# An attention and top-2 expert kernel on one core: 24 expert blocks moved under the gating of the last token groups, with a table of their own, and a smaller mask

## The chip, the cores and the metric

The kernel runs on one core of a Trainium2 chip. The core has a matrix engine (TensorE, PE in the views), VectorE (DVE), ScalarE (ACT), GpSimd (POOL) and SyncE (SP, which here only issues transfers). They run unsynchronised and meet through semaphores. Matmuls write to PSUM, everything else lives in SBUF or in device memory. The metric is the device time of the whole program in microseconds, lower is better; the number compared is the median of several runs.

## The reference

Only what matters here is left in. 128 sequences of 64 tokens, width 128, so 8192 tokens.

```python
def attention(q, k, v, mask, ...):            # q = layernorm(x), k = v = ctx
    qp = (q + pe) @ Wq.T + bq; kp = (k + pe) @ Wk.T + bk; vp = v @ Wv.T + bv    # 16 heads of 8
    scores = jnp.einsum('bhqd,bhkd->bhqk', qh, kh) * d_head ** (-0.5)
    m = mask[:, None, None, :] | causal[None, None, :, :]
    scores = scores - m.astype(scores.dtype) * 10000000.0
    out = softmax(scores) @ vh
    return out @ Wo.T + bo

def ffn(x, ...):                              # x = layernorm(x1)
    probs = softmax(gelu(x @ wg1 + bg1) @ wg2)          # 8 experts
    top_vals, top_idx = jax.lax.top_k(probs, 2)
    h = gelu(einsum('nd,edh->enh', x, w_in))            # 128 -> 256
    o = einsum('enh,ehd->end', h, w_out)                # 256 -> 128
    return einsum('ne,end->nd', gates, o)

x = x + attention(...)
x = x + ffn(layernorm(x))
```

## The kernel before

It has two phases. The **attention phase** walks over 64 tiles of 128 tokens (`NT`), in 16 stages (`NS`) of four tiles. For a tile, PE makes the scores of all 16 heads in two PSUM banks and adds the mask (`scores`, L377 and L383), DVE takes the row maxima (L776) and subtracts them (L780), ACT exponentiates (L620), PE transposes the probabilities (L393), ACT copies them out (L678), PE multiplies by the values (L406, L411), DVE divides (`normalise`, L788, L790), PE applies Wo (`project_o`, L420) and DVE adds the residual (L798). Each engine has one hand-written order: for every stage a `body` with steps u = 0 to 3, in which the work of other stages is slotted. Two to three stages later the same bodies do the **gating** of a group (the four tiles of a stage r): layer norm, transposes (`transpose_rows`, L444), hidden layer (`gate_hidden`, L450), Gelu (L668), logits (L456), softmax (L672, L830 to L832), the two largest experts (`find_two_largest`, `select`), the rank of each token among those of its pair of experts (`rank_tokens`, L463 to L470), the running counts (`count_tokens`, L865, L869) and the row number of each token (`positions`). POOL then scatters the group's rows (`scatter_rows`, L1136, four DMAs) into `routed_rows` in device memory. That buffer has one region for each of the 28 pairs of experts.

When the last two groups (14 and 15) are through, the final counts are copied (`tails`, L1026). From them SP and ACT each write 14 paddings of 128 rows behind the ends of the regions (`pad_regions`, L231 loads the addresses into registers, L238 issues), and `make_tables` on DVE works out for each block of 128 rows where it begins and which two experts it needs.

The **expert phase** runs over 91 blocks (`NB`, a static bound). SP loads each block of rows (`load_group`, L330, up to `RX` = 8 blocks ahead), PE transposes it (L553), PE does the up projection (L562) from the weights that ACT has copied to a fixed place (L732), ACT applies Gelu (L717), PE does the down projection (L573), DVE combines with gates and residual (L1055, L1059), POOL scatters the result to the output (L1174). PE's order in the loop is up(b+1), transposes(b+2), down(b). The mask of a stage is loaded to 128 partitions with all eight sequences of the stage for each of them (L260) and made into `negmask` by one DVE instruction over 128x512 elements (L770), although each partition belongs to one sequence of each tile only. It is added with four matmuls of 64x64, one for each quarter of the array.

```python
for half in range(2):
    r = slice(half * 64, half * 64 + 64)
    for b in range(2):
        last = nc.tensor.matmul(S_bank[half][b * L:(b + 1) * L, :]..., spread_s[r, r],
                                negmask[r, par, 2 * u + b, :]..., start=False, stop=True)
```

## Time and profile before

| | us |
|---|---|
| median of 3 runs | 621.63 (619.68 to 622.26) |
| the profiled execution | 623.75 |
| its span, first to last instruction | 622.0 |
| attention phase and last gating, to the final counts | 0 to 411.3 |
| paddings, tables, first block on its way | 411.3 to 432.4 |
| expert phase | 432.4 to 622 |

The profiled execution lies 2.1 us above the median, and 1.75 us of it are outside the span. The page gives PE 81% busy over the span, DVE 77%, ACT 63%, POOL 40%, but these are averages over phases with different limits: in the page's slices DVE shows nines through the attention phase, PE shows nines through the expert phase, and between them both fall to zero while the DMA engines are at their busiest. The granted TensorE clock is 9 in nearly all slices and 5 in the three slices of the transition.

### The profile page before, as it was taken

Reading aid. Unit: us, or ns where it says so; the run is one execution under the profiler, and the core shown is the slowest. Engines: PE = TensorE matmul, PEld = TensorE weight load, DVE = VectorE, ACT = ScalarE, POOL = GpSimd, SP = SyncE. Lnnn points to the kernel's source line nnn. Section 1 sums busy time; section 2 is a strip of 40 time slices with the busy share of each in tenths; the row PEclk is TensorE's granted clock in tenths of the full one; section 3 lists DMA queues with packets and bytes.
Section 4 is the critical chain, followed back from the end, with each engine's and each line's share of the span. In section 5 each row is a group of like instructions: output and inputs, shape, how many; then the busy total and the mean of one; then the engine's idle time right before and its main releaser. Section 6 shows DMA issues by size and latency. Waiting matters only on the chain.

```text
span 622.0 us, 18994 instructions
## 1 busy us (share of the span) xinstructions
PE 501.8 (81%) x6640; PEld 377.4 (61%) x6640; DVE 481.1 (77%) x1629; ACT 393.0 (63%) x723; POOL 248.8 (40%) x323
## 2 busy tenths in 40 slices
PE   2579898888888888888888887411999999999992
PEld 0146555555554554554555554301999999999992
DVE  3588999999999999999999997660566666566662
ACT  2156687777777777777777676511666666566660
POOL 4131233353353354254254233340355555455552
PEclk9999999999999999999999999555999999999997
DMA  3137212212212212212110101047233334333310
GB/s 110 18 81 220 62 48 69 78 42 66 81 40 65 83 39 65 83 40 62 46 41 26 52 20 38 35 137 241 76 107 103 109 105 110 98 110 86 80 42 1
DMA packets 41805, 46.87 MB, mean 75 GB/s; under 512 B 9738, under 2 KB 33555, under 8 KB 41248
## 3 DMA queue, kind: packets, MB, share of 16 engines
q1 hardware_dynamic: 33696, 30.39, 18.7%
q0 software_dynamic: 5984, 12.90, 6.1%
q10 hardware_dynamic: 2032, 2.36, 1.3%
q8 instruction: 55, 0.90, 0.6%
q14 instruction: 38, 0.31, 0.2%
HBM read 28.54 MB, written 18.58 MB: 76 GB/s over the span
## 4 chain that ended last, share of the span: by engine, by line
DVE 35%; PE 34%; issue 13%; SPq 9%; DMA 2%; ACT 2%; POOL 1%; ACTq 0%; another core or an unknown queue 0%; POOLq 0%; DVEq 0%
PE probs_t L562 14%; PE bank L573 13%; DVE smax L776 9%; DVE rden L788 7%; SPq L266 5%; DVE rows L798 2%; PE scores L553 2%; DVE left L843 2%; DVE sm L780 1%; SPq L238 1%; DVE stat L753 1%; DVE stat L804 1%; DVE xT L763 1%; PE scores L377 1%; PE probs_t L393 1%
## 5 line engine op out<-in xcount | busy, mean ns | idle before, releaser
L1174 POOL DMA_INDIRECT out<-yb,token_row x91 | 89.3, 982 | 106.2 <-DVE yb L1059 65.9
L1136 POOL DMA_INDIRECT routed_rows<-rows,pos x64 | 64.3, 1004 | 122.5 <-DVE pos L879 100.9
L678 ACT ACTIVATE pt<-probs_t 128x1024 f32<-128x1024 f32 x64 | 65.5, 1023 | 60.0 <-PE probs_t L393 59.7
L717 ACT ACTIVATE hb<-probs_t 128x512 f32<-128x512 f32 x91 | 54.3, 597 | 73.2 <-PE probs_t L562 54.9
L562 PE MATMUL probs_t<-xbT,wi 128*128 128x128 f32 x728 | 98.1, 278 | 2.3 <-ACT wi L732 1.2
L377 PE MATMUL scores<-kx,qT 64*64 64x512 f32 x512 | 70.6, 621 | 36.2 <-DVE sm L780 23.9
L573 PE MATMUL bank<-wo,hb 128*128 x728 | 96.1, 275 | 0.0
L562 PEld LDWEIGHTS probs_t<-xbT,wi 128*128 128x128 f32 x728 | 90.1, 195 | 3.1 <-issue 1.7
L573 PEld LDWEIGHTS bank<-wo,hb 128*128 128x128 f32 x728 | 88.5, 192 | 0.1
L776 DVE TENSOR_REDUCE smax<-scores 128x16 f32<-128x1024 f32 x64 | 77.8, 1216 | 12.2 <-PE scores L383 10.9
L780 DVE TENSOR_TENSOR sm<-scores,smax 128x1024 f32<-128x1024 f32 x64 | 78.4, 1224 | 2.2
L1055 DVE SCALAR_TENSOR_TENSOR part<-bank,gate,xb 128x128 f32<-128x128 f32 x91 | 31.8, 350 | 59.4 <-issue 32.1
L732 ACT COPY wi<-wi_all 128x256 f32 x182 | 63.8, 401 | 18.6 <-issue 18.6
L393 PE MATMUL probs_t<-ident_s,sm 128*128 128x128 f32 x512 | 67.3, 274 | 1.3 <-ACT sm L620 1.3
L620 ACT ACTIVATE sm<-sm 128x1024 f32<-128x1024 f32 x64 | 67.3, 1051 | 0.2
L788 DVE RECIPROCAL rden<-bank 128x128 f32<-128x128 f32 x64 | 60.1, 940 | 2.3 <-remote 2.0
L393 PEld LDWEIGHTS probs_t<-ident_s,sm 128*128 128x128 f32 x512 | 57.2, 141 | 5.6 <-issue 4.9
L406 PEld LDWEIGHTS bank<-pt,vx 128*32 128x32 f32 x2048 | 32.0, 109 | 45.6 <-DVE onT L790 29.2
L406 PE MATMUL bank<-pt,vx 128*32 128x64 f32 x2048 | 41.9, 222 | 18.1 <-DVE onT L790 7.8
L377 PEld LDWEIGHTS scores<-kx,qT 64*64 64x64 f32 x512 | 13.8, 132 | 69.0 <-DVE sm L780 41.3
L411 PE MATMUL bank<-pt,ones_s 128*32 128x128 f32 x1024 | 43.2, 275 | 0.6 <-issue 0.5
L1035 DVE COPY xbT<-scores 128x128 f32<-128x128 f32 x91 | 26.0, 286 | 20.2 <-PE scores L553 18.5
(117 smaller groups left out, 838.3 us busy)
## 6 DMA issues: line engine op xcount, KB each, us to landing
xb<-routed_rows SPq DMA_DIRECT2D x91, 132.5 KB
ctx_in<-ctx_t SPq DMA_DIRECT2D x16, 256.0 KB, 3.0
x_all<-x SPq DMA_DIRECT2D x16, 256.0 KB, 3.3
kx<-kT SPq DMA_DIRECT2D x256, 16.0 KB
routed_rows<-padding_rows SPq DMA_DIRECT2D x15, 132.5 KB
routed_rows<-padding_rows ACTq DMA_DIRECT2D x14, 132.5 KB
out<-yb,token_row POOLq DMA_INDIRECT x91
mask_in<-mask SPq DMA_DIRECT2D x16, 64.0 KB, 3.8
```

What stands on the lines that cost most here:

```text
L377: nc.tensor.matmul(S_bank[half][b * L:(b + 1) * L, :].rearrange("p (h k) -> p h k", k=L), qT[r, par, o:o + L], kx[r, par, :, o:o + L], sta ...
L393: last = nc.tensor.transpose(PT_bank[j // 4][:, (j % 4) * P:(j % 4 + 1) * P], pr[:, j * P:(j + 1) * P], ident[:, :])
L406: nc.tensor.matmul(XB[g * VB:(g + 1) * VB, b * L:(b + 1) * L], v[:, c:c + VB], pt[:, 2 * g + j, b * L:(b + 1) * L], start=(j == 0 and b == ...
L562: last = nc.tensor.matmul(UBK[b % 2][:, (2 * j + c) * BLK:(2 * j + c + 1) * BLK], wi[:, b % RH, j, c * P:(c + 1) * P], xbT[:, b % RH, :], ...
L573: last = nc.tensor.matmul(DBK[b % 2][:, j * D:(j + 1) * D], hb[:, b % RH, 2 * j + c, :], wo[:, bass.ds(experts[j], 1), c, :].rearrange("p ...
L620: nc.scalar.activation(sm[:, u % 2, :, :], sm[:, u % 2, :, :], ACT.Exp).then_inc(s_exp, 1)
L678: nc.scalar.activation(pt[:, :, :].rearrange("p j q -> p (j q)"), PT2[:, :], ACT.Copy).then_inc(s_ptev, 1)
L776: nc.vector.reduce_max(smax[:, :], S2[:, :].rearrange("p (h k) -> p h k", k=L), AX).then_inc(s_max, 1)
L780: nc.vector.tensor_tensor(sm[:, u % 2, :, :], S2[:, :].rearrange("p (h k) -> p h k", k=L), smax[:, :].unsqueeze(2).broadcast_to([P, H, L]) ...
L788: nc.vector.reciprocal(rden[:, :], XB[:, P:2 * P]).then_inc(s_rden, 1)
L1136: nc.gpsimd.indirect_dma_start(out=rows_d, out_offset=bass.IndirectOffsetOnAxis(ap=pos[:, r % RR, u:u + 1], axis=0), in_=rows[:, r % RR, u ...
L1174: nc.gpsimd.indirect_dma_start(out=out, out_offset=bass.IndirectOffsetOnAxis(ap=token_row[:, b % RY:b % RY + 1], axis=0), in_=yb[:, b % RY ...
```

## The change

**The first 24 blocks come early.** After group 12 is counted there are enough rows in `routed_rows` for at least 24 full blocks, whatever the input. In stage 15 DVE makes a first table from the counts so far, rounded down to full blocks (`blocks_of_bins(0)`, `ends_of_bins(0)`, `bins_of_blocks(0)`, `write_tables(0)`, `start_second_part`); PE turns it (`turn_table(0)`). The expert loop then starts after the hidden layer of group 14, and the rest of the gating of groups 14 and 15 is written into the loop by block number (`last_gates(b)` on PE, ACT and DVE; `SCATTER_AT` on POOL). The second table, of 67 blocks, follows at blocks 11 to 14. The number of blocks stays 91.

**The paddings** are all issued by SP, 14 before the loads of blocks 16 to 19 and 14 before those of blocks 20 to 23 (`PADS_BEFORE`), after `tails`, which DVE copies at block 10.

**The mask** is loaded with two DMAs a stage, each to 64 partitions, and kept once: `negmask` is 128x256, and two full matmuls of 128x128 by 512 columns add it.

**Around it**: x is kept in a ring of six stages instead of whole, `RX` goes from 8 to 10, `RY` from 6 to 10, at the end of the attention `normalise(63)` on DVE and `project_o(63)` on PE go ahead of other work.

```diff
+EARLY = 13
+NA = 24
+PART_OF = (0, NA)
+NBS = (NA, NB - NA)
+PADS_BEFORE = (4, 5)
-RX = 8
+RX = 10
-RY = 6
+RY = 10
+SCATTER_AT = (4, 12)
...
-                    sp.dma_start(mask_in[:, s % RING, :, :], mask[s * 2 * U:(s + 1) * 2 * U, :].partition_broadcast(P)
-                                 ).then_inc(s_m[s % RING], 16)
+                    for b in range(2):
+                        src = mask[s * 2 * U:(s + 1) * 2 * U, :].rearrange("(u b) k -> b u k", b=2)[b]
+                        sp.dma_start(mask_in[b * L:(b + 1) * L, s % RING, :, :], src.partition_broadcast(L)
+                                     ).then_inc(s_m[s % RING], 16)
...
-                sp.wait_ge(s_tails, 1)
-                pad_regions(mybir.EngineType.SP, sp, PAD_SP)
-                sp.wait_ge(s_tabd, 1)
                 for g in range(len(GROUPS)):
+                    if g in PADS_BEFORE:
+                        if g == PADS_BEFORE[0]:
+                            sp.wait_ge(s_tails, 1)
+                        half = PADS_BEFORE.index(g)
+                        pad_regions(range(half * NP // 2, (half + 1) * NP // 2))
                     load_group(g)
...
                     for half in range(2):
-                        r = slice(half * 64, half * 64 + 64)
-                        for b in range(2):
-                            last = nc.tensor.matmul(S_bank[half][b * L:(b + 1) * L, :].rearrange("p (h k) -> p h k", k=L),
-                                                    spread_s[r, r], negmask[r, par, 2 * u + b, :].unsqueeze(1).broadcast_to([L, HH, L]),
-                                                    start=False, stop=True)
+                        last = nc.tensor.matmul(S_bank[half][:, :].rearrange("p (h k) -> p h k", k=L), spread_s[:, :],
+                                         negmask[:, par, u, :].unsqueeze(1).broadcast_to([P, HH, L]),
+                                         start=False, stop=True)
...
+                def last_gates(b):
+                    if b == 0:
+                        pe.wait_ge(s_res, NT)
+                        gate_logits(NS - 2)
+                    if b == 3:
+                        pe.wait_ge(s_rge, NS - 1)
+                        transpose_rows(NS - 1)
+                        pe.wait_ge(s_lsh, NS - 1)
+                        rank_tokens(NS - 2)
+                    if b == 5:
+                        gate_hidden(NS - 1)
+                    if b == 7:
+                        pe.wait_ge(s_pch, CNT * (NS - 2) + 2)
+                        gate_logits(NS - 1)
+                    if b == 10:
+                        pe.wait_ge(s_lsh, NS)
+                        rank_tokens(NS - 1)
+                    if b == 13:
+                        turn_table(1)
...
+                def last_gates(b):
+                    if b == 0:
+                        gate_exp(NS - 2)
+                        ln2_norm(NS - 1)
+                    if b == 3:
+                        xt2_evac(NS - 1)
+                    if b == 5:
+                        gate_gelu(NS - 1)
+                    if b == 7:
+                        gate_exp(NS - 1)
...
-                act.wait_ge(s_tails, 1)
-                pad_regions(mybir.EngineType.Activation, act, PAD_ACT)
...
+                def last_gates(b):
+                    if b == 0:
+                        choose(NS - 2)
+                    if b == 3:
+                        count_tokens(NS - 2)
+                        positions(NS - 2)
+                    if b == 7:
+                        choose(NS - 1)
+                    if b == 10:
+                        count_tokens(NS - 1)
+                        dve.wait_ge(s_pch, CNT * (NS - 1) + 2)
                         nc.vector.tensor_copy(tails[:, :], run_s[:, :]).then_inc(s_tails, 1)
+                        positions(NS - 1)
+                    if b == 11:
+                        blocks_of_bins(1)
+                        ends_of_bins(1)
+                    if b == 12:
+                        bins_of_blocks(1)
+                    if b == 14:
+                        write_tables(1)
```

Where instructions stand, at the places that matter. On **SP**, before the change, the last paddings are followed by the register load of the first four blocks' addresses and the loads of blocks 0 to 3 (`ISA` rows move an address from a register; `xb<-routed_rows` is the load of a block):

```order
L238 DMA routed_rows<-padding_rows 16x2120
L318 TENSOR_LOAD row_table
L330 ISA
L330 DMA xb<-routed_rows 128x265
```

In the changed kernel, blocks 0 to 15 are loaded first. These are the rows from the end of the first 14 paddings over block 16 to 19 to the second register load of counts:

```order
L326 DMA routed_rows<-padding_rows 16x2120
L333 TENSOR_LOAD row_table
L346 ISA
L346 DMA xb<-routed_rows 128x265
L346 ISA
L346 DMA xb<-routed_rows 128x265
L346 ISA
L346 DMA xb<-routed_rows 128x265
L346 ISA
L346 DMA xb<-routed_rows 128x265
L319 TENSOR_LOAD tails
```

What moved: the paddings stood ahead of every block load, and stand now ahead of block 16 and, after these four loads, once more ahead of block 20. The shape of a padding transfer is the same on both sides.

On **ACT**, before the change, the gating of group 15 ends, the paddings follow (L238), and then the loop begins; these are the rows up to the first padding (`ex` is the exponential of the logits, `rows` the normed rows of a group, `hid_s` the hidden layer's Gelu):

```order
L672 ACT_TABLE_LOAD
L672 ACTIVATE ex<-lg 128x32
L641 ACTIVATE rows<-rows,shift,rstd 128x128 x4
L643 ACTIVATE rows<-routing_s 128x4
L662 ACTIVATE xt<-bank 128x512
L668 ACT_TABLE_LOAD
L668 ACTIVATE hid_s<-bank,bg_s 128x128
L672 ACT_TABLE_LOAD
L672 ACTIVATE ex<-lg 128x32
L231 TENSOR_LOAD tails
```

In the changed kernel the same place reads as follows, from the Gelu of block 0 to that of block 1 (`hb<-probs_t` is a block's Gelu, `wi<-wi_all` a copy of expert weights):

```order
L753 ACTIVATE hb<-probs_t 128x512
L704 ACT_TABLE_LOAD
L704 ACTIVATE ex<-lg 128x32
L673 ACTIVATE rows<-rows,shift,rstd 128x128 x4
L675 ACTIVATE rows<-routing_s 128x4
L770 ISA
L770 COPY wi<-wi_all 128x256
L770 ISA
L770 COPY wi<-wi_all 128x256
L753 ACT_TABLE_LOAD
L753 ACTIVATE hb<-probs_t 128x512
```

What moved: the exponential of group 14 and the layer norm of group 15 stand between the Gelu of block 0 and the weight copies of block 2.

## Rows read from the trace of the kernel before

**Rows 1.** Busy time by stretch: start:end, length, engines, PEclk, DMA share, GB/s.

```profile
84.00:384.00 300.00, 255.84 (x4136) 160.62 (x4133) 288.41 (x848) 226.76 (x360) 118.83 (x172) 1.00 0.19 53
440.00:611.00 171.00, 169.05 (x1512) 168.63 (x1510) 106.75 (x538) 105.07 (x263) 87.39 (x90) 1.00 0.34 93
```

**Rows 2.** Chain that ended last, in the transition: start us, us, what.

```profile
411.46 1.15 SPq L231
...
421.43 0.50 SPq L238
...
422.11 0.50 SPq L238
...
425.50 4.61 DMA routed_rows<-padding_rows
430.27 2.15 DMA xb<-routed_rows
```

**Rows 3.** The same chain in the attention phase: mask on SP, PE and DVE.

```profile
33.13 0.50 SPq L260
...
71.62 0.22 PE scores L383 x4
...
99.54 0.60 DVE negmask L770
```

**Rows 4.** Timeline, end of the attention: start, us, engine line op out<-in [idle before <-releaser].

```profile
388.12 0.96 DVE L788 RECIPROCAL rden<-bank 128x128 f32<-128x128 f32 x1 [1.95 <-remote]
...
395.94 0.77 PE L420 MATMUL bank<-wo_s,onT 128*128 128x128 f32 x2 [0.75 <-DVE onT L790]
...
413.17 1.08 DVE L905 TENSOR_TENSOR cum<-cum 128x28 f32<-128x28 f32 x5
```

**Rows 5.** Timeline of the gating of group 15, and ACT's way into the loop.

```profile
400.22 1.65 ACT L641 ACTIVATE rows<-rows,shift,rstd 128x128 f32<-128x128 f32 x4 [1.30 <-POOL shift L1126]
...
402.11 1.09 PE L444 MATMUL bank<-ident_s,rows 128*128 128x128 f32 x4 [4.38 <-ACT rows L643]
...
403.23 0.60 ACT L662 ACTIVATE xt<-bank 128x512 f32<-128x512 f32 x1 [1.27 <-PE bank L444]
...
403.84 1.28 ACT L668 ACT_TABLE_LOAD   x1
...
405.14 0.37 ACT L668 ACTIVATE hid_s<-bank,bg_s 128x128 f32<-128x128 f32 x1
...
406.82 0.23 ACT L672 ACTIVATE ex<-lg 128x32 f32<-128x32 f32 x1
...
409.69 0.27 DVE L856 TENSOR_TENSOR sel<-code,routing_s 128x112 f16<-128x112 f32 x1
...
425.67 1.42 ACT L732 COPY wi<-wi_all 128x256 f32 x4 [18.62 <-issue]
```

**Rows 6.** Timeline of PE in the expert phase: blocks 0, 1 and 20.

```profile
433.48 2.04 PE L562 MATMUL probs_t<-xbT,wi 128*128 128x128 f32 x8 [0.54 <-DVE xbT L1035]
...
438.02 1.06 PE L573 MATMUL bank<-wo,hb 128*128 x8
...
441.70 0.27 PE L553 MATMUL scores<-ident_s,xb 128*128 128x128 f32 x1
...
472.04 0.27 PE L553 MATMUL scores<-ident_s,xb 128*128 128x128 f32 x1
```

**Rows 7.** Busy time of PE alone by stretch: length, PE (count), PEclk, DMA share, GB/s.

```profile
388.00:390.00 2.00, 0.54 (x36) 0.99 0.19 68
390.00:392.00 2.00, 1.09 (x27) 0.50 0.00 0
...
436.00:438.00 2.00, 1.78 (x9) 0.56 0.02 7
```

**Rows 8.** Instructions by line: duration ns min/median/max, first and last start us.

```profile
L231 SPq TENSOR_LOAD <-tails x2: 1152/1314/1477, 411.5 to 419.8; - x2
...
L318 SPq TENSOR_LOAD <-row_table x23: 295/302/675, 426.1 to 591.8; - x23
...
L722 ACTq TENSOR_LOAD <-expert_table x23: 547/637/787, 425.0 to 599.1; - x23
```

More of the change, by code:

```diff
@@ L44 @@
 RW = 2 * D + E + 1
[L45 removed]
+ROUND = float(3 << 22)
 CH = 9
@@ L226, in build @@
         s_tok, s_part = (sem(n) for n in ("token_rows_ready", "first_expert_added"))
-        PAD_SP, PAD_ACT = range(0, NP // 2), range(NP // 2, NP)
-        def pad_regions(engine, queue, bins):
-            for first in range(bins.start, bins.stop, NP // 4):
-                _, values = nc.values_load_multi_w_load_instructions(
-                    tails[0:1, first:first + NP // 4], engines=[engine], min_val=0, max_val=ROWS - BLK,
-                    skip_runtime_bounds_check_because="made on the chip by counting into existing regions")
-                for k in range(NP // 4):
-                    start = (first + k) * REG
-                    at = nc.s_assert_within(values[k], start, start + N,
-                                            skip_runtime_bounds_check_because="a region holds all tokens")
-                    queue.dma_start(rows_d[bass.ds(at, BLK), :], pad_c.ap()).then_inc(s_pad, 16)
         (s_bt, s_bte, s_up, s_gl, s_dn, s_gm, s_gt, s_yb) = (sem(n) for n in (
@@ L313, in _, with pad_regions @@
                     body(s, s // 2, s % 2)
+                def pad_regions(bins):
+                    for first in range(bins.start, bins.stop, NP // 4):
+                        _, values = nc.values_load_multi_w_load_instructions(
+                            tails[0:1, first:first + NP // 4], engines=[mybir.EngineType.SP], min_val=0, max_val=ROWS - BLK,
+                            skip_runtime_bounds_check_because="made on the chip by counting into existing regions")
+                        for k in range(NP // 4):
+                            start = (first + k) * REG
+                            at = nc.s_assert_within(values[k], start, start + N,
+                                                    skip_runtime_bounds_check_because="a region holds all tokens")
+                            sp.dma_start(rows_d[bass.ds(at, BLK), :].rearrange("(a r) w -> a (r w)", a=16),
+                                         pad_c.ap().rearrange("(a r) w -> a (r w)", a=16)).then_inc(s_pad, 16)
                 def load_group(g):
-                    first, n = GROUPS[g]
+                    p, first, n = GROUPS[g]
+                    if first == PART_OF[p]:
+                        sp.wait_ge(s_tabd, 3 * p + 1)
                     _, values = nc.values_load_multi_w_load_instructions(
@@ L472, in rank_tokens, with turn_table @@
                     last.then_inc(s_rank, 1)
+                def turn_table(p):
+                    pe.wait_ge(s_spread, p + 1)
+                    for k in range(3):
+                        last = nc.tensor.transpose(TABLE[p][:, k * P:(k + 1) * P], spread_out[:, k, :], ident[:, :])
+                    last.then_inc(s_tabp, 1)
                 def body(s, i, par):
@@ L499, in body @@
                             project_v(s + 1)
+                        if u == 2 and s == NS - 1:
+                            turn_table(0)
                         if u == 0:
@@ L736, in _ @@
                 act.wait_ge(s_wo, 32)
-                act.wait_ge(s_tabd, 2)
-                for g, (first, n) in enumerate(GROUPS):
+                for g, (p, first, n) in enumerate(GROUPS):
                     experts = experts_of(g)
@@ L1007, in _ @@
                     body(s, s // 2, s % 2)
+                normalise(NT - 1)
                 residual(NT - 2)
@@ L1164, in body @@
                             add_positions(s + 3)
-                        if u == 3 and runs(s, 3):
+                        if u == 3 and runs(s, 3, NS - 2):
                             scatter_rows(s - 3, (3,))
```

198 lines of the change are left out of this document (104 added, 94 removed).

## The prediction

> **What bounds the kernel now.** I read the busy time by stretch first [rows 1]. From 84 to 384 us DVE is busy 288.4 of 300: the attention phase is DVE-bound once it is under way. From 440 to 611 PE is busy 169.1 of 171: the expert phase is PE-bound, at 1.896 us a block (sixteen blocks lie between the transposes of block 4 at 441.70 and of block 20 at 472.04, which is 30.34 us [rows 6]). Between them the chain of waits [rows 2] runs through SP: the counts are there at 411.46, paddings are issued until 425.99, the last one lands at 430.11, the first block lands at 432.42. PE has nothing to do for these 21 us, and it is thinly busy through the gating before. That hole, 37.5 us from the last `project_o` at 395.94 [rows 4] to the first up projection at 433.48 [rows 6], is the time in which nothing of the expert phase runs. The question is how much of it comes back as waits inside the expert loop.
>
> I sum against the profiled execution: span 622.0, time 623.75, which is 2.1 above the median of 621.63. I carry differences in the span over to the median.
>
> **Attention phase, the mask.** DVE's mask instruction costs 0.60 us of its chain [rows 3]. Half the elements saves 0.26 of it (the full one is 679 ns for 512 columns, a 128-column one on these engines some 0.29, so 256 columns are about 0.42). It is on the DVE-bound path in about 12 stages: -3.1 us. Against it stand two things. SP, which is the chain in the first 64 us, issues one more mask load of about 0.54 (0.50 and the gap [rows 3]) for each of stages 2 to 4: +1.6, up to +3 because the pieces are now 64 bytes. And the four mask matmuls take 0.22 beyond the scores [rows 3], because four 64x64 quarters stream side by side; two full ones stream one after the other, about 0.43. DVE reaches the maxima 1 to 3 us after the scores are done in a steady stage, so this +0.21 a tile is hidden by DVE's other work, except in the four tiles around 70 to 85 us where the chain runs through PE: +0.8. If DVE's cover were gone it would cost 64 x 0.21 = 13 us. Sum: **-0.5**, bounds -3 and +3.
>
> The Trainium skill, page "TensorEngine Tiling (Array Packing)", says that 64x64 mode gives four independent tiles. By that rule this edit gives speed away on PE. The 0.22 in the row agrees; it changes the sum only by the tiles on the PE path.
>
> **Stage 15, the early table.** DVE gets 6 + 5 + 4 small operations at about 0.22 (five took 1.08 [rows 4]) before the last subtraction, with the spread of 384 elements 3.7 us in all, then 1.7 us for writing the tables and starting the second part. The 3.7 lie on DVE's bound path. The 1.7 and part of the rest fall where DVE waits anyway: it stood 1.95 for an unseen cause before the reciprocal at 388.12 [rows 4]. `normalise(63)` now goes ahead of the count, which saves 1.5. Following the order through, the last `project_o` ends at 397.3 instead of 396.7 (395.94 + 0.77), bounds 395 and 399.
>
> **Into the loop.** From there: transposes of group 14 1.09, copy 0.60, table load 1.28, Gelu 0.37 [rows 5], load of eight registers 0.64 [rows 8], two weight copies 0.71 (half of 1.42 for four [rows 5]), and 0.2 of hops: the up projection of block 0 starts at T = **402.2**, not 433.48. That is 31.3 us won so far. The first blocks' rows are ready: POOL's last scatter of group 12 is shifted by the same 3.7 us, to about 390, which is ten ahead of need.
>
> **The loop under the gating.** Without gating, the down projection of block 0 ends 5.6 us after T (439.08 - 433.48 [rows 6], at half clock for the most part) and that of block 10 ends 19.0 later. Now follow ACT, since PE's up(b+2) waits for ACT's weight copies and its down(b+1) for ACT's Gelu.
> - Block 0: ACT waits for down(0), the logits (0.4) and DVE (0.8), then exponential 0.23, layer norm 1.65 + 0.2, copies 0.71, table load 1.28, Gelu 0.60. down(1) starts 6.2 us after down(0) ends instead of 0.95: +5.2. 3.8 us of it leave PE with nothing.
> - Block 3: transposes 1.09, copy 0.60, copies 0.71, Gelu 0.60 and hops: +2.5. Block 5: hidden layer 0.43, Gelu 0.37: +1.4. Block 7: logits, DVE, exponential, copies, table load, Gelu: +3.3, and DVE's choice of experts (2.9 us, from the exponential's end at 407.05 to 409.96 [rows 5]) another 0.2.
> - Clock. The granted clock fell to 0.50 (1.2 GHz) at 390 after PE was busy 0.54 of 2 us, and came back just before 438 (0.56 over 436 to 438) [rows 7], some 4 us after the first up projection. I expect it to fall in block 0's gap: +1.7.
>
> down(10) ends at T + 5.6 + 19.0 + 12.6 + 1.7 = T + 38.9, and rank, count and copy put `tails` at T + 40.4 = 442.6. In the kernel before it was 411.4.
>
> About table loads the Trainium skill ("ScalarE: Activation LUTs", on what ACT_TABLE_LOAD costs) gives 1283 ns and a drain of 1380 ns more for each switch. The rows show 1.28 us between a copy that ended at 403.83 and a Gelu at 405.14, with no drain. By the page the two exposed switches would add 2.8 us.
>
> **The paddings, now in the loop.** This decides it. SP waits for `tails` before it loads block 16. Then 14 paddings: two register loads (1.15 and 1.48 [rows 8]) and 14 issues. With ACT's queue silent, an issue comes every 0.68 us (421.43 to 422.11 [rows 2]), which makes 12.1 us; the row of before, both queues and pauses included, is 14.5 for 14 (411.46 to 425.99). I take 12.9, near the lower end, as the rival queue is gone but not every pause of the first seven need be its doing. Register load and gap 0.4, block 16 is issued at 13.3 and lands 2.15 later [rows 2], at T + 56. PE needs it in iteration 14, about T + 48 after the second table's work on DVE (4 to 5 us over blocks 11 to 14): PE stands some 7 us. After the four loads (1.9) come 14 more paddings, 12.9, and 0.4: block 20 is issued at T + 40.4 + 13.3 + 1.9 + 13.3 = T + 68.9 and lands at T + **71.1** = 473.3. PE has had work for only four blocks in between (8 to 10 us) and stands again for about 5. DVE's table work and one wait are covered by the other; this chain alone sets the time.
>
> Before, PE transposed block 20 at 472.04 [rows 6]. So the chain is **1.3 us behind** the old kernel here, and all 31.3 us are spent. I expect the clock to fall in both waits. The first recovery hides in the second wait, the second one does not: about 5 us at half rate, **+2.5**. Block 24 is loaded about 5 us after block 20 and needed 8 later, so nothing waits from there on, and 70 blocks follow at the old pace with the old tail.
>
> The pages of the skill bear on the paddings too: "DMA: Bandwidth & Descriptors", on issuing engines, says that issuing from several engines saves only the sequencer's issue time. Here issue time is the bound, so giving up ACT's queue costs twice.
>
> Sum: 1.3 + 2.5 = **+3.8**; median 621.6 + 3.8 = **625.4**. Its own range, from the mask's, T's and the paddings' bounds, is 620 to 631.
>
> **Rivals.**
> 1. *Faster: the padding chain is short enough.* If PE keeps 2.4 GHz over the waits (-2.5 and -1.7) and SP issues back to back (0.50 instead of 0.68 for 28 paddings: -5.0, and the pauses -1.6), the sum is -7 and the time 615; half of the slack is enough for -3. It decides at a chain from `tails` to block 20 of 26 us against my 30.7. For it: the issue itself is 0.50 in every row. Against: the same 0.18 gap stands between any two paddings, also alone. Chance 0.24.
> 2. *No clock loss after the waits, rest as forecast*: 625.4 - 2.5 - 1.7 = 621. PE rode through short gaps elsewhere. Chance 0.14.
> 3. *Half clock through the whole gating.* PE is busy half of the time up to block 8. At 1.2 GHz each block costs up to 1.9 more, part of it within ACT's waits: +6 more, and `tails` and all behind it slip: 631. For it: the clock fell at just such a load at 388 to 390 [rows 7]. Chance 0.20.
> 4. *The change doesn't do what it says*: the first loads or the table come so late that the early blocks don't start before the gating ends. Ten us of slack speak against it; it would give 640. Under 0.03, kept within rival 3's tail.
>
> The forecast has 0.42, two thirds of it above the bound of 0.5% (3.1 us, about what a measurement of this kernel can tell from no change). So faster 0.24, same 0.14 + 0.14 = 0.28, slower 0.28 + 0.20 = 0.48. As both signs are likely, the 8-in-10 range goes from rival 1's middle to beyond rival 3: **614 to 636**.
>
> **What the profile after would show.** Block 0's up projection near 402; on ACT the exponential, four norms and a table load between the first two block Gelus, and a 5 us step there; `tails` near 443; PE idle before the transposes of block 16 and again before block 20, released by the loads of `routed_rows`; the transposes of block 20 at 473; clock 0.5 in that stretch; DVE's mask near 0.42. I am wrong if PE doesn't stand there, if `tails` comes before 438, or if paddings are issued faster than every 0.6 us.

## Result and the profile after

| | before | after |
|---|---|---|
| median, us | 620.75 (619.68 to 622.26, 4 runs) | 626.62 (625.42 to 627.89, 4 runs) |
| ratio, 95% interval | 1 | 1.0081 (1.005 to 1.0113) |
| the profiled execution, us | 623.75 | 625.42 |
| its span, us | 622.0 | 623.6 |

The changed kernel is slower by 0.8%. The forecast was 625.4; against the 621.63 that it started from, the difference is +5.0 where +3.8 was expected. Against the median of four runs in the table it is +5.9.

The windows of the changed kernel, to be read against [rows 1] (start:end, length, busy us of PE, weight loads, DVE, ACT, POOL, granted clock as a share of 2.4 GHz, DMA share, GB/s):

```profile
84.00:384.00 300.00, 266.71 (x4073) 160.82 (x4069) 288.03 (x864) 231.17 (x364) 121.77 (x175) 1.00 0.20 53
476.00:611.00 135.00, 135.00 (x1208) 134.93 (x1207) 84.45 (x425) 83.65 (x209) 68.94 (x71) 1.00 0.32 90
```

Nothing has changed in what bounds the two phases. DVE has 288.0 of 300 us in the attention phase, and from 476 on PE never stops. The time is decided between 396 and 476. PE's timeline there, with the last `project_o`, the first up projection, the waits on ACT up to block 9 and the two long ones (start, us, engine line op out<-in, then in brackets the idle time before it and what ended it):

```profile
396.88 0.80 PE L436 MATMUL bank<-wo_s,onT 128*128 128x128 f32 x2 [0.79 <-DVE run_s L907]
...
401.63 2.07 PE L592 MATMUL probs_t<-xbT,wi 128*128 128x128 f32 x8 [0.75 <-ACT wi L770]
...
412.08 2.08 PE L592 MATMUL probs_t<-xbT,wi 128*128 128x128 f32 x8 [3.46 <-ACT wi L770]
...
421.35 1.16 PE L592 MATMUL probs_t<-xbT,wi 128*128 128x128 f32 x8 [1.06 <-ACT wi L770]
...
426.84 1.16 PE L592 MATMUL probs_t<-xbT,wi 128*128 128x128 f32 x8 [1.08 <-ACT wi L770]
...
432.98 1.16 PE L592 MATMUL probs_t<-xbT,wi 128*128 128x128 f32 x8 [1.94 <-ACT wi L770]
...
434.98 1.15 PE L603 MATMUL bank<-wo,hb 128*128 x8 [0.73 <-ACT hb L753]
...
457.77 0.48 PE L583 MATMUL scores<-ident_s,xb 128*128 128x128 f32 x1 [7.81 <-DMA xb<-routed_rows]
...
473.57 0.48 PE L583 MATMUL scores<-ident_s,xb 128*128 128x128 f32 x1 [5.41 <-DMA xb<-routed_rows]
```

The last `project_o` is at 396.88 (before 395.94 [rows 4]) and the first up projection at 401.63 (before 433.48 [rows 6]), so 31.85 us are won there. The last row is the transposes of block 20: 473.57, where the kernel before has 472.04 [rows 6]. All of it is gone again. The SP timeline shows what held PE at the last two rows:

```profile
442.59 11.66 SPq L326 DMA_DIRECT2D routed_rows<-padding_rows  x14
454.86 2.04 SPq L346 DMA_DIRECT2D xb<-routed_rows  x4
458.58 11.84 SPq L326 DMA_DIRECT2D routed_rows<-padding_rows  x14
470.99 4.82 SPq L346 DMA_DIRECT2D xb<-routed_rows  x8
```

Fourteen paddings, four loads, fourteen paddings, loads: one queue, with nothing but the loads of addresses into registers between them, from the moment the counts are there. The rows of block 16 are asked for at 454.86 and PE begins with them at 457.77; those of block 20 at 470.99 and 473.57.

### The profile page after: what moved, and what is told of

The parts are those of the page before. It is cut to its first block, busy times and chain, and to the rows that moved or that the text cites. A ratio compares the mean times of both kernels' runs of the same rounds, so it can differ in the third digit from the quotient of the medians.

```text
span 623.6 us, 18779 instructions
## 1 busy us (share of the span) xinstructions
PE 521.9 (84%) x6515; PEld 384.0 (62%) x6515; DVE 480.8 (77%) x1651; ACT 392.7 (63%) x723; POOL 248.6 (40%) x323
## 4 chain that ended last, share of the span: by engine, by line
DVE 36%; PE 30%; issue 15%; SPq 12%; DMA 2%; ACT 1%; POOL 1%; ACTq 1%; POOLq 0%; DVEq 0%
PE probs_t L592 12%; PE bank L603 12%; DVE smax L814 10%; DVE rden L826 8%; SPq L267 5%; SPq L326 3%; DVE rows L836 2%; PE scores L583 2%; DVE stat L842 2%; DVE left L881 1%; DVE stat L791 1%; DVE xT L801 1%; SPq L319 1%; DMA bq_s<-bq 1%; DVE mv L847 1%
## 5 line engine op out<-in xcount | busy, mean ns | idle before, releaser
L592 PE MATMUL probs_t<-xbT,wi 128*128 128x128 f32 x728 | 101.3, 284 | 10.9 <-ACT wi L770 9.1
L603 PE MATMUL bank<-wo,hb 128*128 x728 | 100.3, 283 | 0.7 <-ACT hb L753 0.7
L592 PEld LDWEIGHTS probs_t<-xbT,wi 128*128 128x128 f32 x728 | 92.5, 199 | 12.6 <-ACT wi L770 11.6
L603 PEld LDWEIGHTS bank<-wo,hb 128*128 128x128 f32 x728 | 92.3, 199 | 1.2 <-issue 1.0
L395 PEld LDWEIGHTS scores<-kx,qT 64*64 64x64 f32 x512 | 13.9, 133 | 68.1 <-DVE sm L818 43.5
L646 ACT ACTIVATE vx<-bank 64x256 f32<-64x256 f32 x64 | 24.2, 379 | 30.6 <-PE bank L381 30.1
```

The source lines that it names most:

```text
L395: nc.tensor.matmul(S_bank[half][b * L:(b + 1) * L, :].rearrange("p (h k) -> p h k", k=L), qT[r, par, o:o + L], kx[r, par, :, o:o + L], sta ...
L592: last = nc.tensor.matmul(UBK[b % 2][:, (2 * j + c) * BLK:(2 * j + c + 1) * BLK], wi[:, b % RH, j, c * P:(c + 1) * P], xbT[:, b % RH, :], ...
L603: last = nc.tensor.matmul(DBK[b % 2][:, j * D:(j + 1) * D], hb[:, b % RH, 2 * j + c, :], wo[:, bass.ds(experts[j], 1), c, :].rearrange("p ...
```

## The experiments

The kernel before was timed again beside each set: 621.9 for the first, 619.63 for the second (`gates_spread`, `best2`), 620.78 for the third (`late_act`, `act_ten`). Ratios are to the kernel before, timed in the same set; where a time is set against that of a kernel of another set, the two were not timed side by side.

### The mask alone

`mask_only` is the kernel before with the two mask loads, the 128x256 `negmask` and the two full matmuls, and nothing else of the change.

```diff
-                    sp.dma_start(mask_in[:, s % RING, :, :], mask[...].partition_broadcast(P)).then_inc(s_m[s % RING], 16)
+                    for b in range(2):
+                        sp.dma_start(mask_in[b * L:(b + 1) * L, s % RING, :, :], src.partition_broadcast(L)
+                                     ).then_inc(s_m[s % RING], 16)
...
-                        for b in range(2):
-                            last = nc.tensor.matmul(..., spread_s[r, r], negmask[r, par, 2 * u + b, :]..., stop=True)
+                        last = nc.tensor.matmul(..., spread_s[:, :], negmask[:, par, u, :]..., stop=True)
```

> The kernel before with the new mask alone (two loads of 64 partitions a stage, 128x256 on VectorE, two full matmuls a tile). The prediction's sum for this part was -0.5 us: 620. The trace of the changed kernel suggests more: its last mask instruction starts 2.1 us later than in the kernel before (355.6 against 353.5), so the other theory is +2 us: 622.8, with a start-up some 3 to 5 us longer (the keys of stage 2 land at 69.5 instead of 66.3) that VectorE's 0.27 us a stage gives back only in part.

Measured: 621.56 (12 runs), ratio 0.9991 (0.997 to 1.0012). The edit is neutral; the bounds are a gain of 0.3% and a loss of 0.1%, or -1.9 and +0.7 us, so that of the two theories -0.5 fits and +2 doesn't. On its chain of waits (start, us, what) the two full matmuls show the forecast's weakest number:

```profile
71.10 0.55 PE scores L383 x2
...
75.37 0.54 PE scores L383 x2
```

Two full ones take 0.54 on the chain where four quarters took 0.22 [rows 3]. In PE's busy time over 84 to 384 us it is 268.3 against the 255.8 of [rows 1]. The summary of DVE's mask line (min/median/max ns, first and last start), in the kernel before and in this one:

```profile
L770 DVE SCALAR_TENSOR_TENSOR negmask<-mask_in,causal_s x16: 678/679/1716, 15.1 to 353.5; 128x512 f16<-128x512 uint8 x16
```

```profile
L770 DVE SCALAR_TENSOR_TENSOR negmask<-mask_in,causal_s x16: 411/414/1449, 15.8 to 354.6; 128x256 f16<-128x256 uint8 x16
```

DVE's instruction is shorter by 0.265 us, yet the last of the sixteen starts 1.1 later: what DVE wins, SP's start and PE's tiles at 71 to 87 us take. DVE copies the counts at 408.70 all the same, 2.5 us sooner than in the trace of the kernel before (411.25). That trace has a wait of 1.95 before a reciprocal [rows 4]; here, with DVE's order unchanged, the same reciprocal starts at once:

```profile
385.98 0.96 DVE L788 RECIPROCAL rden<-bank 128x128 f32<-128x128 f32 x1
```

### Paddings one group later

`pads_5_6` is the changed kernel with the 28 paddings moved behind one more group of loads.

```diff
-PADS_BEFORE = (4, 5)
+PADS_BEFORE = (5, 6)
```

> The changed kernel with the two halves of the paddings one group later each (ahead of blocks 20 and 24 instead of 16 and 20). Theory (the chain of SP's issues after the counts sets when PE goes on): the wait before block 16 goes away, block 20 is there in time, and PE waits once, before block 24, whose rows land near 474.5 instead of a start at 482.7: -8 us, 618.4. Rival (the gating inside the loop is what costs, SP's queue is covered): no change, 626.6.

Measured: 621.22, ratio 0.999 (0.9964 to 1.0016), span 619.1: about 5 us below the changed kernel, in the direction forecast, 3 less than forecast. PE no longer stands before block 16, 0.61 before block 20 and 8.78 before block 24. The chain just ahead of block 24:

```profile
471.51 2.55 DMA routed_rows<-padding_rows
...
474.22 2.16 DMA xb<-routed_rows
...
476.42 0.47 PE scores L583
```

The missing 3 us are in two places. Block 24 starts 6.4 sooner than in the changed kernel (476.42 against 482.78), not 8.2, and behind it the span is 1.9 longer (142.7 against 140.8), with the clock at 0.50 over 470 to 480. As for the first, block 24 is the first of the second part, whose loads must wait until the last padding has landed (2.55); in the changed kernel block 20 needs no such wait. So the chain moved past one group and took on a landing.

### Seven paddings on ACT's queue

`pads_act` is `pads_5_6` with 7 paddings on SP before group 5, 14 before group 6, and 7 on ACT's queue, one at a block from block 12 on.

```diff
-PADS_BEFORE = (4, 5)
+PADS_BEFORE = (5, 6)
+SP_PADS = (range(0, 7), range(7, 21))
+ACT_PADS = range(21, 28)
+ACT_PADS_FROM = 12
```

> As pads_5_6, but 7 of the 28 paddings are issued by ScalarE, one each at blocks 12 to 18 between its Gelu and its weight copies; SP issues 7 ahead of block 20 and 14 ahead of block 24. Theory (SP's issue time is the bound): the rows of block 24 land near 467, PE waits 2 us at most: -16 us against the changed kernel, 611, faster than the kernel before by 1.6%. Rival (the paddings' transfer itself is the bound, not the issue): no better than pads_5_6, 618. Each padding on ScalarE may cost 0.2 to 0.8 us in blocks 12 to 18.

Measured: 614.51 (8 runs), ratio 0.9907 (0.9873 to 0.994), span 611.9. That is 3.5 above the 611 of the theory and as much below the 618 of the rival. The chain:

```profile
464.11 2.90 DMA routed_rows<-padding_rows
...
467.16 2.10 DMA xb<-routed_rows
...
469.31 0.33 PE scores L585
```

Block 24 comes 7.1 us sooner than in `pads_5_6` (476.42), and the median falls by 6.7. In the trace the miss is 2.3 at block 24 itself (469.31 for 467, so that PE waits 3.21 and not 2 at most) and 1.8 behind it, where the clock is 0.50 over 470 to 472 and 0.74 in the 2 us after. Only the queue that issues seven of the paddings and their order were changed, and seven issues of 0.68 and their register load of about 1.6 are 6.4. So it is the issue time on SP, not the transfers, that makes the chain.

The Trainium skill ("DMA: Bandwidth & Descriptors", section "Issuing engines are not separate DMA queues") says of spreading transfers over engines that it only saves issue time of the sequencer. The rows agree in kind: the transfers themselves got no faster (2.90 and 2.10 against 2.55 and 2.16). But "only" hides that the issue time can be all there is to win.

### The clock after the waits

`warm` is the changed kernel with small matmuls that compute nothing of the result, written to a free part of a bank, to keep PE busy in the two waits.

```diff
+WARM = {14: 110, 18: 75}
...
+                        if b in (14, 18):
+                            for _ in range(WARM[b]):
+                                nc.tensor.matmul(YB[:, 0:P], ones16[:, :], ones16[:, :], start=True, stop=True)
```

> The changed kernel with idle work for PE in the two waits: 110 small fp16 matmuls of ones before the transposes of block 16, 75 before those of block 20, whose result nobody reads. Theory (the half clock after the second wait costs, as the prediction had it with 2.5 us, the trace of the changed kernel shows 1.6): the clock stays at 1.00, block 20 starts at the same 473.5, and what follows is 1.6 us sooner. Rival: the clock does not matter there or the filler itself delays block 20; then no gain or a loss of 1 to 3 us.

Measured, in a single execution: 625.32, span 623.5. First the changed kernel, PE alone by stretch (length, PE busy, granted clock, DMA share, GB/s), then `warm`:

```profile
472.00:474.00 2.00, 0.42 (x2) 0.85 0.75 213
474.00:476.00 2.00, 2.00 (x11) 0.50 0.67 188
476.00:478.00 2.00, 2.00 (x17) 0.80 0.54 147
```

```profile
474.00:476.00 2.00, 1.14 (x8) 1.00 0.83 242
476.00:478.00 2.00, 2.00 (x20) 1.00 0.67 184
```

With the small matmuls in the two waits PE is idle for 1.32 and 1.98 us instead of 7.81 and 5.41, and the granted clock stays at 1.00. From the transposes of block 20 to the end of the span it is 148.6 us (623.5 - 474.86) against 150.0 (623.6 - 473.57): the half clock costs 1.4, where the forecast had 2.5. `warm` is one execution, but the traces of `mask_only`, `best2`, `late_act` and `act_ten`, which have no wait of PE before block 20, also give 148.4 to 148.7 for this stretch.

That `warm` is not faster for it has its own reason. Its code is the changed kernel's up to block 14, but its counts are ready at 443.25 instead of 441.27, though its first up projection was earlier (399.75 against 401.63). The way between took 43.5 instead of 39.6 us. Its clock ahead of any dummy matmul:

```profile
412.00:414.00 2.00, 2.00 (x11) 0.50 0.00 0
414.00:416.00 2.00, 2.00 (x12) 0.50 0.00 0
...
434.00:436.00 2.00, 1.73 (x8) 0.50 0.00 0
...
438.00:440.00 2.00, 2.00 (x12) 0.50 0.08 33
```

And the changed kernel's own:

```profile
396.00:398.00 2.00, 1.22 (x6) 0.50 0.78 213
...
412.00:414.00 2.00, 1.92 (x9) 0.50 0.01 4
...
434.00:436.00 2.00, 1.27 (x12) 1.00 0.08 33
```

Both are at half clock from before the loop on, to about 406 in `warm` and 408 in the changed kernel, and again behind block 0's gap. The wait of 1.94 before block 9's up projection is the same in both; after it the clock is 0.50 in `warm` and 1.00 in the changed kernel, and 2.7 of the 3.9 us come from there on, the other 1.2 from a longer stretch at half clock behind block 0's gap. So a part of rival 3 happened in one execution and not in the other. `late_act`, `act_ten` and `gates_spread` show it once more: after a wait of 1.24 before the up projection of block 8 the clock is 0.50 over 424 to 426 in the first and stays at 1.00 in the other two.

### The gating placed where its inputs are ready

`gates_spread` leaves the paddings as in the changed kernel and moves the gating: each step of groups 14 and 15 comes where its input is ready, and the last count after block 7 instead of block 10; POOL's scatters of the two groups go with it, from blocks 4 and 12 to 2 and 9. On ACT, whose order matters most:

```diff
                 def last_gates(b):
-                    if b == 0:
-                        gate_exp(NS - 2)
+                    if b == 1:
                         ln2_norm(NS - 1)
                     if b == 3:
                         xt2_evac(NS - 1)
+                    if b == 4:
+                        gate_gelu(NS - 1)
                     if b == 5:
-                        gate_gelu(NS - 1)
-                    if b == 7:
                         gate_exp(NS - 1)
...
+                        if b == 2:
+                            gate_exp(NS - 2)
                         if b > 1:
                             gelus(b - 2)
```

On PE the logits of group 14 go ahead of up(0), ranks after block 1, group 15's transposes, hidden layer, logits and ranks after blocks 2, 3, 4 and 7. DVE chooses group 14's experts before block 0's gates.

> The changed kernel, with only the places of the last two groups' gating moved: logits of group 14 ahead of the first up projection, its exponential ahead of the first block Gelu, its choice of experts ahead of the first block's gates; group 15's steps after blocks 1 to 5, its ranking after block 7 instead of 10, the second table after blocks 8 to 11. The order is such that ACT finds every input ready. The paddings stay before groups 4 and 5. My theory: the four ACT stalls of the changed kernel (3.5, 1.1, 1.1 and 2.7 us of PE idle) and the three blocks of delay are what puts the tails at 441.3; without them the last count is at about 427 (first down projection at 405.8, seven blocks at 1.9, a slow clock for some of them, and 2 for rank and count). Everything behind hangs on that chain of SP, so the transposes of block 20 come at about 460 instead of 473.6, and the time is 613 (612 to 616), 13 below the changed kernel. Rival: the clock or DVE sets the early blocks; then the tails gain only the moved blocks, some 5 us, and the time is about 621. Second rival: the time behind block 20 does not hang on this chain; then it stays at 626.

Measured: 613.17, ratio 0.9885 (0.9837 to 0.9933). DVE's copy of the counts, and PE before block 20:

```profile
L1099 DVE CAST tails<-run_s x1: 180/180/180, 427.6 to 427.6; 128x28 uint32<-128x28 f32 x1
```

```profile
459.73 0.48 PE L581 MATMUL scores<-ident_s,xb 128*128 128x128 f32 x1 [7.32 <-DMA xb<-routed_rows]
```

Counts at 427.6 (427 expected, 441.3 in the changed kernel), block 20 at 459.7 (460 expected, 473.57), time 613 (613 expected, 626.6). Both fell by almost the same: 13.7 at the counts, 13.8 at block 20, 13.4 in the median. PE still stands 7.3 us there, so the padding chain is as long as before; it only starts sooner. Of the 13.7, three blocks less before the count are 5.7 (at 1.9 a block), and the other 8.0 are ACT's stalls and the half clock behind the first of them. Not all of these are gone: PE still waits for ACT 0.73 and 1.24 around the up projection of block 8.

### Both together, and a new wait

`best2` has the gating of `gates_spread`, the paddings of `pads_act` but on ACT from block 10, and 14 row buffers instead of 10 (what these give alone, no run tells).

```diff
-PADS_BEFORE = (4, 5)
-RX = 10
+PADS_BEFORE = (5, 6)
+SP_PADS = (range(0, 7), range(7, 21))
+ACT_PADS = range(21, 28)
+ACT_PADS_FROM = 10
+RX = 14
```

> The gating placed as in gates_spread, and the paddings spread: 7 on SP before group 5, 14 on SP before group 6, 7 on ACT's queue one per block at blocks 10 to 16, with 14 row buffers instead of 10. My theory: after the tails (427) SP needs 5.8 for seven paddings, 3.6 for the loads of group 5, 11.5 for fourteen paddings, 2.9 for the last to land and 2.1 for the rows of block 24: its transposes come at about 454 (469.3 in pads_act), where PE would need them at 452.5, so that chain and PE end together and the expert phase runs almost without a wait from 402 on. Time 599 (596 to 603), ratio 0.964. Rival: spread paddings only pay once; with the gating's gain, PE or DVE becomes the bound in blocks 2 to 20 (gating, second table and blocks share DVE) and the time is 606 or more.

Measured: 605.55, ratio 0.9764 (0.9715 to 0.9812): 6.5 above the forecast, and nearly at the rival's 606. A part of that is a wait that neither had named. Its ACT and PE timelines show it:

```profile
422.38 0.71 ACT L787 COPY wi<-wi_all 128x256 f32 x2
429.28 0.64 ACTq L763 DMA_DIRECT2D routed_rows<-padding_rows  x1
430.02 0.60 ACT L770 ACTIVATE hb<-probs_t 128x512 f32<-128x512 f32 x1 [6.93 <-issue]
```

```profile
430.76 1.15 PE L603 MATMUL bank<-wo,hb 128*128 x8 [3.37 <-ACT hb L770]
431.75 1.74 PE L592 MATMUL probs_t<-xbT,wi 128*128 128x128 f32 x8
...
433.50 1.91 PE L603 MATMUL bank<-wo,hb 128*128 x8
```

ACT's queue reads its part of the counts, which come at 427.35, ahead of the Gelu of block 8. Everything behind that on ACT waited too, PE stood 3.4 us, and the next matmuls ran at half clock (1.91 for a down projection instead of 1.06).

`late_act` changes one number of it, `act_ten` moves three more paddings from SP to ACT as well.

```diff
-ACT_PADS_FROM = 10
+ACT_PADS_FROM = 12
```

> best2 with one number changed: ACT's seven paddings begin at block 12 instead of block 10. In best2 ACT, in its order ahead of the Gelu of block 8, waits for the tails and loads seven registers (it stands 6.9 us before that Gelu, PE 3.4 of it), and the granted clock falls to half for the blocks behind. My theory: this wait is all that stood between 605.5 and the forecast; gates_spread, which has no such wait, transposes block 12 at 433.45 against 436.57. So block 12 comes 3.1 us sooner, block 24 at 458.2 (461.3), its rows lie ready at 457, and the time is 602.3 (601 to 604). Rival: the padding chain on SP is what holds blocks 20 to 24; then block 24 stays near 461 and the time is 605.5.

Measured: 601.04 (599.61 to 601.74), ratio 0.9665 (0.9631 to 0.9698), where 602.3 (601 to 604) was expected. Block 12 comes at 434.00 instead of 436.57, block 24 at 458.58 instead of 461.32, and PE waits for no load of rows any more: those of block 24 land at 457.01. Block 24 comes 2.7 sooner and the span is 2.7 shorter (599.7 against 602.4), so that much is what the wait cost in the traces; the medians, of two sets, differ by 4.5. The rest of `best2`'s miss is of the rival's kind, early blocks that are slower than forecast: PE was to need block 24 at 452.5, and gets there at 458.58. From the first up projection to block 20 these 20 blocks take 49.7 us, in the kernel before 38.6. The longest waits of PE between 404 and 485 us are these:

```profile
423.29 1.67 PE L592 MATMUL probs_t<-xbT,wi 128*128 128x128 f32 x8 [1.24 <-ACT wi L787]
...
433.04 1.13 PE L592 MATMUL probs_t<-xbT,wi 128*128 128x128 f32 x8 [1.26 <-ACT wi L787]
```

```diff
-SP_PADS = (range(0, 7), range(7, 21))
-ACT_PADS = range(21, 28)
+SP_PADS = (range(0, 7), range(7, 18))
+ACT_PADS = range(18, 28)
```

> late_act with ten of the 28 paddings on ACT's queue instead of seven (blocks 12 to 21, two register loads of five), and 11 instead of 14 on SP before group 6. My theory: the last padding of SP lands 2.4 us sooner, but that chain no longer ends last, so nothing is won: same as late_act within 1 us, or up to 1.5 slower by ACT's three issues and second register load (0.9 to 1.7 us) ahead of a block Gelu. Rival: the chain still ends last at block 24; then the time is 2 us below late_act.

Measured: 601.08 (600.27 to 601.65), ratio 0.967 (0.9639 to 0.9702), the same as `late_act`. It is a weaker test than it looks: SP's paddings end 3.1 us sooner (449.48 against 452.61), but the load of block 24 is issued only 0.7 sooner (454.15 against 454.89), for a cause that I did not find. That the chain on SP no longer ends last is shown by `late_act`'s trace, in which PE doesn't wait for it; `act_ten` agrees. With 601.0 both are 19.7 us below the kernel before, and 25.6 below the changed one (of another set).

## Why the prediction was right

The mechanism is as forecast: the counts come late, one queue issues everything behind them, PE stands twice, and block 20 starts 1.5 us behind the kernel before. That the median agrees to 1.2 us is in part luck, as two errors of opposite sign behind block 20 show below.

**T, the start of the loop.** 402.2 was forecast, 401.63 measured; the last `project_o` ended at 397.7 (396.88 + 0.80) against 397.3. The fifteen small DVE operations of the early table take 0.18 to 0.24 us each, where 0.22 was taken, and writing the tables 1.5 for 1.7. The way from `project_o` into the loop took 3.95 instead of 4.9, as the transposes of group 14 start before it ends (397.47).

**The gating in the loop.** Forecast T + 40.4 for the counts, measured 441.27, which is T + 39.6. The stall at block 0 is as described. ACT's timeline:

```profile
404.35 1.28 ACT L704 ACT_TABLE_LOAD   x1
409.56 0.23 ACT L704 ACTIVATE ex<-lg 128x32 f32<-128x32 f32 x1 [3.93 <-DVE lg L860]
409.70 1.63 ACT L673 ACTIVATE rows<-rows,shift,rstd 128x128 f32<-128x128 f32 x4
411.24 0.19 ACT L675 ACTIVATE rows<-routing_s 128x4 f32<-128x4 f32 x1
411.33 0.69 ACT L770 COPY wi<-wi_all 128x256 f32 x2
412.04 1.28 ACT L753 ACT_TABLE_LOAD   x1
413.34 0.60 ACT L753 ACTIVATE hb<-probs_t 128x512 f32<-128x512 f32 x1
```

Exponential, four norms, copies, table load, Gelu, in this order; PE's 3.46 idle was forecast as 3.8. `gates_spread` confirms the term from the other side: without most of the stalls the counts come 8.0 sooner, and 5.7 more by the three blocks.

The steps of the loop are read from one up projection to the next, less the 1.9 of an undisturbed block: +1.9 at block 3 (forecast 2.5, which took the transposes at 1.09, their length at half clock, where they took 0.60), +1.6 at block 5 (1.4) and +3.3 at block 7 (3.5, which comes as a wait of 1.94 and one of 0.73). At block 0 down(1) starts 5.8 after down(0) ends (6.2). The clock was placed wrongly. It was forecast to fall in block 0's gap and to cost 1.7. The trace has it at 0.50 from 396 on, ahead of the loop, so that down(0) ends at T + 6.7 instead of T + 5.6. Behind the gap 0.6 is lost. That the two make 1.7 again is chance, as up(2), at half clock as well, lies within the 5.8. All in all down(10) ends at T + 38.4 for T + 38.9.

The first table load stands at once behind the Gelu of block 0, while the exponential starts 3.9 us after the end of the load, when its logits are there. The load does not wait for them, so it costs nothing there; the second one, ahead of block 1's Gelu, is exposed. The copies end at 412.02, the load takes 1.28, the Gelu begins at 413.34. The Trainium skill ("ScalarE: Activation LUTs", section "What ACT_TABLE_LOAD costs") adds a drain of about 1380 ns to the 1283 of the load. The trace shows the 1283 and 0.02 behind it, no drain. As an estimate from the page's figure, the counts would have come at about 444 with the two exposed loads.

**The paddings.** From the counts (441.27) to the load of block 16 (454.86) it is 13.6, forecast 13.3; the four loads take 2.0, forecast 1.9; from their end at 456.9 to the load of block 20 at 470.99 it is 14.1, forecast 13.3; from there to PE's start 2.6, forecast 2.15. The chain is 32.3 us long instead of 30.7, and it began 1.3 sooner than forecast, so the two errors nearly cancel: PE's waits are 7.8 and 5.4, forecast as about 7 and 5, and block 20 comes at 473.57, forecast at 473.3. Of the 1.6 that the chain is longer, 0.6 is in the second fourteen paddings and 0.4 in the landing; the first fourteen with their two register loads take 12.8, forecast 12.9. One padding of the second set held the queue 1.31 instead of 0.50:

```profile
466.38 1.31 SPq L326
```

The register loads vary most:

```profile
L319 SPq TENSOR_LOAD <-tails x4: 942/1544/1737, 441.5 to 463.2; - x4
```

Four of them, seven addresses each, take 0.9 to 1.7 us, 5.8 in all, where 5.3 was taken. The pace of 0.68 was read off a row of the kernel before in which ACT's queue was not silent (it issued its own paddings until 424.89). It came out right all the same: with ACT silent the issues of the changed kernel follow at 0.68 as well, at 444.80, 445.48 and 446.16, so in these rows a second queue takes paddings off this one but does not change its pace.

The step on which all hung, that giving the 28 paddings to one queue makes issue time the bound, is shown by `pads_act` and `late_act`: taking seven off SP's chain is worth 7 us as long as that chain ends last, and in `late_act`, where it doesn't, PE no longer waits for it.

**The clock after the waits.** The mechanism was right, the size not: 2.5 forecast, 1.4 measured by `warm`. The term that was mis-sized is "about 5 us at half rate". The rows show 0.50 over 474 to 476 and 0.80 over the next 2 us, some 3 us at half rate from the first matmul at 473.57 on. After the first wait it was more, 5.4 us (from 457.77 to about 463), and this one was hidden in the second wait, as forecast.

**Behind block 20.** The forecast gave the changed kernel 2.5 us more than the kernel before from here on. It has 0.07 more: from the transposes of block 20 to the end of the span it is 150.03 after and 149.96 before, although the half clock costs 1.4 of it now. The kernel before lost that much once later:

```profile
538.95 1.13 PE L562 MATMUL probs_t<-xbT,wi 128*128 128x128 f32 x8 [1.24 <-ACT wi L732]
```

No such wait stands in any of the other nine traces. From block 30 to block 90 they have 113.8 to 114.1, `mask_only` with the same loop among them, and the kernel before 115.2. Why it came there is not known; no run tells. So the two profiled executions differ by +1.7 (625.42 - 623.75), where the sum had +3.8. The medians differ by +5.0, because the profiled execution of before lay 2.1 above its median and that of after lies 1.2 below its own. The forecast carried a difference of spans over to a median; it came out well for the median, but by an error of 2.1 in the span and one of 3.3 in the carrying, of opposite sign. That is luck.

What was carried over wrongly can be named in part. The trace that the sum started from has two waits that no other trace has, the 1.95 before the reciprocal at 388.12 and these 1.24; the profiled execution of `mask_only`, without either, has a span of 619.3, 4.3 below the changed kernel's. Of the 27 executions of the kernel before in the first set, 23 are shorter than the profiled one. The changed kernel has such a spread too, as the 43.5 us of `warm` for the way to the counts show, against 39.6. Which waits the unprofiled executions had is not recorded, so this explains the spread and does not show it run by run.

**The mask.** Forecast -0.5 with bounds of -3 and +3, measured alone -0.6 with an interval of -1.9 to +0.7 (from the ratio). In the parts it was less right than in the sum. The mask matmuls on PE's path cost 0.54 instead of 0.43, and SP's two mask loads of a stage are 0.68 and 0.64, each with a gap of 0.05, where 0.54 was taken for each with its gap:

```profile
33.19 0.68 SPq L261
33.92 0.64 SPq L261
```

The keys of stage 2 land at 69.5, 3.2 us later than before, a little beyond the upper end of what was given, and the sixteenth mask instruction starts 2.1 later (355.56 against 353.47). That the last `project_o` is then only 0.9 later is due to stage 15: the kernel before stands 1.95 before a reciprocal for a cause that the trace does not name [rows 4], and the changed one doesn't. It was not the shifted DVE order that removed it, as `mask_only` has the old order and doesn't stand there either; whether the smaller mask did, or whether the wait belongs to that one execution, is open. With the parts sized as measured the sum would have been +0.8 (-3.1 for DVE, three stages at 0.88 on SP, four tiles at 0.32 on PE), at the edge of what `mask_only` allows.

**The rivals.** Rival 1 asked for a chain of 26 us from the counts to block 20; it took 32.3, as issues followed at 0.68 and not at 0.50. Its point, that the early blocks pay where the chain is short, is shown by `pads_act` and `late_act`, which shorten it by other means. Rival 2 lost, as the clock fell in both waits. Rival 3 has the clock low in the gating; the profiled run had it so from before the loop to 408 and from 412 to about 415, `warm` for a further 7 us from 433 on. It was given as all or nothing, and it comes in pieces.

## What to carry to other kernels

Work that is taken out of a hole and laid under a loop does not vanish: it delays the event that the hole was waiting for, here the final counts by 30 us, and everything that can only start then meets the loop. So follow the late event, not the busy share; ask what is issued after it, on how many queues, and at which iteration the loop needs it. Then place each step of the interleaved work where its inputs have been ready for one iteration, so that the engine that feeds the loop never waits inside it, and let a queue read a late value only after it is surely there: `best2` lost 2.7 us by the traces, and 4.5 between medians, by reading it two blocks too soon.

## What the runs showed of the hardware

- A padding DMA with its address in a register holds SP's queue for 0.50 us as a rule (up to 1.31 in the changed kernel), and another 0.18 passes to the next, with ACT's queue issuing or silent. A load of seven addresses into registers takes 0.9 to 2.0 us on SP over the runs here, and it is paid on the chain once per seven DMAs.
- Four 64x64 matmuls on the four quarters of the array took 0.22 us on the chain behind the scores, two full ones of 128 rows with the same 512 columns 0.54. Over the whole span PE is busy 26.0 us with the first and 40.0 with the second, so a mask with half the elements was dearer for PE.
- The table load of ACT runs ahead of the wait for data of the instruction that it belongs to, and takes 1.28 us with nothing behind it (404.35, 3.93 us ahead of its exponential; 412.04 to 413.32, and the Gelu at 413.34).
- With PE kept busy by small matmuls through most of a wait of 8 and of 5 us the granted clock stayed at 1.00, where it fell to 0.50 without them; the second fall cost 1.4 us. After a wait of 1.94 us it was 0.50 in one trace and 1.00 in another, at the same instruction, and so after one of 1.24.
